# Keys of elements 0 and 1 and the values of element 0 of the third stage computed between the first attention and the FFN; the first gelu ahead of the last copy of transposed probabilities

## The reference

```python
x = x + _L0_xattn_ref(_layernorm(x), ctx_1024, ctx_1024, ...)      # 16 heads of 8, causal
x = x + _L0_ffn_ref(_layernorm(x), w_up, w_down)                   # 128 -> 512 -> 128, ternary weights, gelu
x = x + _L1_xattn_ref(_layernorm(x), ctx_1024, ctx_1024, mask, ...) # 16 heads of 64, relative positions
x = x + _L1_ffn_ref(_layernorm(x), rhs)                            # int8 product, 128 x 128
```

```python
hq = (q @ Wq).reshape(Bq, Lq, D_K, N_HEADS)
hk = (k @ Wk).reshape(Bq, Lk, D_K, N_HEADS)      # keys: from the context alone
hv = (v @ Wv).reshape(Bq, Lk, D_V, N_HEADS)      # values: from the context alone
attn = jnp.einsum('bidn,bjdn->bijn', hq, hk)
attn = attn + jnp.take_along_axis(b_full, idx[None, :, :, None], axis=2)   # relative positions
out = jnp.einsum('bijn,bjdn->bidn', softmax(attn), hv)
```

## Time and profile before

| what | value |
|---|---|
| median of 3 runs | 449.82 us (449.65 to 452.0) |
| span of the profiled execution | 447.1 us |
| mean granted clock of TensorE | 0.977 |
| PE busy | 412.8 us (92%) |
| DVE busy | 380.6 us (85%) |
| ACT busy | 377.9 us (85%) |
| POOL busy | 252.8 us (57%) |
| PE's share of the chain that ended last | 71% |

### The profile page before, as it was taken

How to read it: one execution, slowest core, us unless ns; L and a number is a source line. 1 busy time by engine, 2 the same in 40 slices (tenths; PEclk the granted TensorE clock), 3 DMA queues, 4 the chain that set the end, 5 groups by cost and what they waited for, 6 DMA issues and landing times.

```text
span 447.1 us, 16738 instructions
## 1 busy us (share of the span) xinstructions
PE 412.8 (92%) x6147; PEld 313.4 (70%) x6147; DVE 380.6 (85%) x1236; ACT 377.9 (85%) x1483; POOL 252.8 (57%) x370
## 2 busy tenths in 40 slices
PE   8999999998789998999999999999999999998771
PEld 6555565654457677877788888877888887887560
DVE  5799999989758984697779999998999999899954
ACT  1999999998945565599999999999999999999851
POOL 4388888887967651023345454644745555365765
PEclk9999999999979999999999999999999999999796
DMA  7250000000000002999667667666757847772000
GB/s 215 60 195 25 15 7 11 11 8 15 2 0 2 0 2 74 241 215 217 141 146 172 151 144 171 150 131 153 167 134 152 192 118 164 153 171 53 6 8 23
DMA packets 54392, 44.88 MB, mean 100 GB/s; under 512 B 43952, under 2 KB 49328, under 8 KB 54320
## 3 DMA queue, kind: packets, MB, share of 16 engines
q1 hardware_dynamic: 53616, 43.59, 41.1%
q10 hardware_dynamic: 704, 0.32, 0.3%
HBM read 22.92 MB, written 20.97 MB: 98 GB/s over the span
## 4 chain that ended last, share of the span: by engine, by line
PE 71%; DVE 17%; ACT 5%; issue 3%; POOL 2%; DMA 1%; SPq 1%; POOLq 0%; ACTq 0%; DVEq 0%
PE PS L1003 61%; PE PS L1213 4%; PE PS L1019 3%; PE PS L1179 1%; DMA wr<-in_wr 1%; DVE relr L753 1%; ACT prob L523 1%; DVE nmax L705 1%; DVE nmax L707 1%; POOL prob L320 1%; DVE relw L748 1%; DVE nmax L676 1%; DVE probT L683 1%; PE PS L1169 1%; DVE nmax L770 1%
## 5 line engine op out<-in xcount | busy, mean ns | idle before, releaser
L377 POOL TENSOR_TENSOR prob<-prob,rsum 128x480 f32<-128x480 f32 x64 | 66.4, 1057 | 83.1 <-DVE rsum L903 59.7
L523 ACT ACTIVATE prob<-prob,nmax 128x120 f32<-128x120 f32 x256 | 100.2, 417 | 1.8 <-DVE nmax L923 1.8
L439 ACT ACTIVATE prob<-PS,nmax 128x120 f32<-128x120 f32 x256 | 89.6, 393 | 4.2 <-DVE nmax L770 2.5
L320 POOL TENSOR_TENSOR prob<-prob,rsum 128x480 f32<-128x480 f32 x64 | 62.5, 988 | 22.8 <-DVE rsum L743 12.7
L439 ACT ACTIVATION_READ_ACCUMULATOR prob<-PS,nmax 128x1 f32 x256 | 61.2, 239 | 0.0
L523 ACT ACTIVATION_READ_ACCUMULATOR prob<-prob,nmax 128x1 f32 x256 | 56.8, 222 | 0.0
L1003 PE MATMUL PS<-xnT,wq 128*128 128x128 f32 x288 | 43.1, 286 | 2.2 <-ACT xnT L591 1.1
L1003 PE MATMUL PS<-rT,qv 64*32 64x152 f32 x2048 | 40.7, 292 | 2.5 <-issue 2.2
L1003 PE MATMUL PS<-probT,hv 120*64 120x128 f32 x512 | 36.0, 284 | 6.8 <-ACT probT L608 4.4
L1003 PE MATMUL PS<-ctx,wk 128*128 128x120 f32 x288 | 41.1, 279 | 0.0
L1003 PEld LDWEIGHTS PS<-probT,hv 120*64 120x64 f32 x512 | 28.0, 139 | 18.3 <-issue 8.0
(11 more groups left out here) (191 smaller groups left out, 1082.1 us busy)
## 6 DMA issues: line engine op xcount, KB each, us to landing
rel_scratch<-relw SPq DMA_DIRECT2D x128, 152.0 KB, 2.6
relr<-rel_scratch SPq DMA_DIRECT2D x64, 240.0 KB, 4.6
ctx<-in_ctxT SPq DMA_DIRECT2D x32, 60.0 KB, 1.9
out_x<-fin SPq DMA_DIRECT2D x16, 64.0 KB, 4.0
x_all<-in_x SPq DMA_DIRECT2D x1, 640.0 KB, 7.1
wr<-in_wr SPq DMA_DIRECT2D x1, 512.0 KB, 5.4
wq<-in_wq SPq DMA_DIRECT2D x1, 512.0 KB, 3.7
wk<-in_wk SPq DMA_DIRECT2D x1, 512.0 KB, 4.5
```

Source lines behind the costliest of these rows:

```text
L320: return pool.tensor_tensor(pr, pr, cols(rsum[p], g, HG).unsqueeze(2).to_broadcast([S, HG, SK]), ALU.mult)
L377: return pool.tensor_tensor(pr, pr, cols(rsum[p], g, HG).unsqueeze(2).to_broadcast([S, HG, SK]), ALU.mult)
L439: last = act.activation(cols(prob[p], n, SK), cols(scores, q, SK), ACT.Exp, bias=nmax[p][:, n:n + 1], accum_out=ssum[p][:, n:n + 1])
L523: last = act.activation(cols(pr, n, SK), cols(pr, n, SK), ACT.Exp, bias=bias[:, n:n + 1], accum_out=total[:, n:n + 1])
```

## The change

`made_early(t)` is true for elements 0 and 1. For these the key products and both copies of the keys leave `layer1`, and for element 0 the value products and copies leave it too. They are placed in `attn0(16)`, `ffn0(0)` and `attn0(17)` of the crossing, in banks that are free there (keys of element 0 in banks 2 and 3, of element 1 in banks 0 and 3; values in banks 1 and 3). Of the six copies of keys and values made there, three are on DVE and three on ACT. On ACT the gelu of FFN element 0 now stands inside `attn0(17)`, ahead of the copy of the last transposed probabilities. SP waits for `cap` as well before it loads a context and a mask, because the values of element 0 no longer tell it that the buffer is free. The core of the diff:

```diff
+        def made_early(t):
+            return isinstance(t, int) and t < 2
...
@@ SP, layer1
                     after(sp, A1["hv_ps"], 2 * t - 2)
+                    after(sp, A1["cap"], t - 1)
...
@@ ACT, attn0, ahead of the copy of probT_ps 2t+2 of element s-2
+                if at_step(s, NB + 1):
+                    act.wait_ge(A1["hv_ps"], 2)
+                    act.activation(cols(hv[0], 0, 512), PS[0:SK, 3, :], ACT.Copy).then_inc(A1["hv0"], 1)
+                    ffn0(0, 0)
+                    act.wait_ge(A1["hk_ps"], 3)
+                    act.activation(cols(kT[1], 1, 4 * SK), PS[:, 0, 0:4 * SK], ACT.Copy).then_inc(A1["kT1"], 1)
@@ ACT, crossing
                 ffn0(-1, 1)
+                act.wait_ge(A1["hv_ps"], 1)
+                act.activation(cols(hv[0], 1, 512), PS[0:SK, 1, :], ACT.Copy).then_inc(A1["hv1"], 1)
                 attn0(17, 1)
-                ffn0(0, 0)
                 attn0(18, 0)
@@ DVE, attn0, between the reciprocals of rsum
+                    if at_step(s, NB):
+                        dve.wait_ge(A1["hk_ps"], 1)
+                        dve.tensor_copy(cols(kT[0], 1, 4 * SK), PS[:, 2, 0:4 * SK]).then_inc(A1["kT1"], 1)
@@ DVE, attn0, ahead of the copy of oT
+                if at_step(s, NB):
+                    dve.wait_ge(A1["hk_ps"], 2)
+                    dve.tensor_copy(cols(kT[0], 0, 4 * SK), PS[:, 3, 0:4 * SK]).then_inc(A1["kT0"], 1)
+                if at_step(s, NB + 1):
+                    dve.wait_ge(A1["hk_ps"], 4)
+                    dve.tensor_copy(cols(kT[1], 0, 4 * SK), PS[:, 3, 0:4 * SK]).then_inc(A1["kT0"], 1)
@@ PE
+            def key_half(t, h, bank):
+                for m in range(4 * h, 4 * h + 4):
+                    last = mm(PS[:, bank, (m % 4) * SK:(m % 4 + 1) * SK], cols(wk1_sb, m, 2 * DK), ctx_sb[t][:, :])
+                last.then_inc(A1["hk_ps"], 1)
+            def value_half(t, h, bank):
+                mm(PS[0:SK, bank, :], ctx_sb[t][:, :], cols(wv1_sb, h, 512)).then_inc(A1["hv_ps"], 1)
@@ PE, attn0, after the product with wo
+                if at_step(s, NB):
+                    pe.wait_ge(attn1_loaded, 16 * 11)
+                    pe.wait_ge(A1["ctx_loaded0"], 16)
+                    pe.wait_ge(A0["probs"], 62)
+                    key_half(0, 1, 2)
+                if at_step(s, NB + 1):
+                    pe.wait_ge(A1["ctx_loaded1"], 16)
+                    pe.wait_ge(F0["xnT"], 1)
+                    key_half(1, 1, 0)
@@ PE, attn0, after the transposes of groups 2 and 3
+                if at_step(s, NB + 1):
+                    pe.wait_ge(A1["hv0"], 1)
+                    key_half(1, 0, 3)
@@ PE, attn0, between the two halves of probT x vexp
+                if at_step(s, NB):
+                    pe.wait_ge(A0["probs"], 64)
+                    key_half(0, 0, 3)
@@ PE, attn0, after the second half of probT x vexp
+                if at_step(s, NB):
+                    value_half(0, 1, 1)
@@ PE, ffn0, after the up product
+                if at_step(s, 0):
+                    pe.wait_ge(A1["kT0"], 1)
+                    value_half(0, 0, 3)
@@ PE, layer1 (four places, and the copies of ACT and DVE likewise)
-                    for m in range(4, 8):
+                    if not made_early(t):
+                        for m in range(4, 8):
```

More of the change, by code:

```diff
@@ L1306, in layer1 @@
                     freed(pe, (A1["relw2"], t + 2, t + 1), (A1["kT1"], t + 1, t))
[L1307 to L1309 removed]
+                    if not made_early(t):
+                        for m in range(0, 4):
+                            last = mm(PS[:, 4, (m % 4) * SK:(m % 4 + 1) * SK], cols(wk1_sb, m, 2 * DK), ctx_sb[p][:, :])
+                        last.then_inc(A1["hk_ps"], 1)
                 t, p = s - 4, par
```

33 lines of the change are left out of this document (19 added, 14 removed).

## The result

| | before | changed |
|---|---|---|
| median of 20 runs each | 449.9 us (447.24 to 455.26) | 452.47 us (451.12 to 457.0) |
| ratio to before | | 1.0066, 95% interval 1.0046 to 1.0087 |
| span of the profiled execution | 447.1 us | 451.6 us |
| its granted clock | 0.977 | 0.977 |

The changed kernel is slower by 0.66%. The forecast was 449.3 us and "within 0.5%"; 452.47 us lies above its range. The profiled execution of the changed kernel took 453.43 us, 1.8 us more than its span, and in every execution with both numbers on record the difference is 1.75 to 1.89 us. So the 2.7 us that I took for what lies around the program was wrong: the profiled execution of before took about 448.9 us, 1 us less than the median, and the profiled one of the changed kernel 1 us more than its own.

The account below looks back on a forecast made before the run. PE was taken to bound the crossing and the third stage's long middle, perhaps with `relw` transfers in its first steps. Span 447.1 + 0.5 - 1.0 = 446.6 us, plus 2.7 us, gave 449.3 us; range 448.0 to 452.0 us.

Parts of the forecast that it names:

- the third-stage term: First steps of the third stage: content products of element 1 start 1.0 us earlier, passed on to the end.
- My bounds: Third-stage gain: 0.1 us if the load at 197.25 us holds PE, 2.1 us if PE's lead is kept whole.
- the loads hold the third stage: Rival for the third stage: loads set the pace, gain only 0.1 us, time 450.2 us; chance 0.1.
- The crossing term: Between attention and FFN: 4.57 us of added PE work on the chain costs +0.5 us, with the clock at 2.4 GHz.
- POOL's wait: Crossing: element 15's transposes wait for POOL's scaling, which let PE start at 124.78 us; PE now comes at 125.13 us.
- the key group: Crossing: each group of key products on PE's chain was priced at 0.89 us at full clock.
- My upper bound: Crossing cost at full clock: +1.5 us, from 0.2 us of wait for each of five groups following a semaphore.
- the second rival: Crossing: the clock fall was absent from timed runs, so 2.2 us more cost, time 451.5 us; chance 0.2.
- the reading of the rows: Crossing: PE's idle pauses of 1.95 us preceded the clock's fall; with work filling them it stays up, giving 449.3 us.

Follow-up runs that it names:

- the filler: Kernel before plus four unread constant products (0.9 us) in PE's pause ahead of the crossing's transposes of element 14; ratios 0.992 and 0.9922 in two runs.
- Crossing only: Changed kernel with unread products of the same shapes put back in the third stage where the moved ones stood; 450.75 us, ratio 1.0012.
- The kernel with this pause filled: Changed kernel plus two unread products of 512 columns in PE's pause ahead of element 2's first position products; 449.79 us, ratio 1.0002.
- the third stage alone: Changed kernel with each moved product group in the crossing cut to one product of 16 or 32 columns; 451.5 us, ratio 1.0023.
- small loads: Changed kernel with only the loads of `relr` for elements 0 and 1 cut to one head in eight; 450.67 us, ratio 1.0022.
- small transfers: Kernel before and changed kernel, each with `relw` stores and `relr` loads of elements 0 and 1 cut to one head in eight; 451.03 and 449.79 us.
- the repeat: Kernel before, unaltered, profiled once more; this execution took 448.87 us, span 447.1 us.
- The two halves alone: Changed kernel with only its crossing products moved in, then with only its third-stage products removed; ratios 1.0012 and 1.0023.

## Why the prediction was wrong

**The failed step is the third-stage term, "-1.0 us, passed on".** Measured at element 2 it is +0.4 to +0.6 us (40.59, 40.65 and 40.76 in three profiles of the changed code against 40.17 and 40.18 us), an error of 1.5 us. Before's code with the filler was once at 40.17 and once at 40.59 us, so the sign of 0.4 us is weak; that there is no gain of 1.0 us is clear. Two assumptions fell.

I let the position products of element 2 start 0.5 us earlier, because I kept the landings of `relr` at their old times. They started 0.2 us later: 21.55 us after the first query products, where before has 21.37. DVE's line 999 started on the landing of a load at 189.94 us, 19.25 us after those products, where its line 974 started at 18.77 us before, because SP issued the load's pair 1.3 us later, behind a store whose last packets had stood behind a transfer of instructions. Crossing only has the same lateness with all its products in place (0.9 us at element 2), so this part of the loss is not owed to the products that I had moved out of the stage.

And I took PE's pause ahead of those products (I had written 1.2 us; it is 2.46 us) as free of cost, when a pause of 1.95 us had brought half clock 70 us earlier in my own argument. The kernel with this pause filled prices the clock at 0.9 us at element 1. It also shows that the gain there need not be passed on: with `ctx` late, element 2 gives nothing back. My bounds, 0.1 to 2.1 us of gain, did not reach a loss at all, and the rival "the loads hold the third stage" had the wait, with the clock missing from it. The gain itself was not invented: 1.74 us of lead at element 0 with the third stage alone, 1.0 us at element 1 with small loads, 3.0 us passed on with small transfers in both kernels.

**The crossing term was right in kind and too small.** Clock 1.00, gelu at nothing, copies in time, POOL's wait met: all as written. From the transposes to the end I had 10.11 us and it was 10.42 us. The term that was too small is the key group: the three on the chain take 0.98 to 1.08 us from start to start here, where I had 0.89 us from the third stage, in which products of the same shape follow; that is 0.47 us more, and the other rows give 0.16 us back. My upper bound had such time as waits.

**The base was not the constant that I made it.** I priced 4.57 us of work at +0.5 us because full clock gives back what half clock took. That holds against an execution with the fall. Against one without it, 7.79 us, the crossing costs 2.63 us. I had this as the second rival, with 2.2 us for the fall, where it measures 1.74 us, and chance 0.2; the repeat shows it true of some executions. How many of the timed ones is not known. What I held against that rival, that span and median agree if 2.7 us lies around the program, was no evidence, since 1.8 us does.

**Not in the sum at all: the long steps of the middle.** They add 1.3 us in the first pair of profiles, 0.8 us in the second (187.07 and 187.27 against 185.74 and 186.48 us). They belong to the program and not to the execution, since they return at the same two steps in four profiles, and they move or vanish with edits elsewhere. The traces tie them to the transfers of instructions: nineteen stalls of nineteen end 1.17 to 1.53 us after a packet of the instruction queue. The Trainium skill, page "Runtime: NRT & Kernel Launch", section "Instruction fetch mechanics", says that each engine's instructions are fetched in blocks ahead of use, which is mostly hidden, and that a taken branch out of the fetched blocks stalls the engine. The trace agrees that there are such transfers, most of them without a stall; here the stalls that do come are 0.4 to 2.0 us long, and whether PE stood still for its next block, and whether the loop's branch has to do with it, no run here decides.

**The sum.** The median is 3.2 us above the forecast. Third stage 1.5, crossing 0.3, middle 0.8 to 1.3, in all 2.6 to 3.1 us. What the executions of before without a fall add would come on top, so it does not close exactly, and a falling clock in the start (1.6 us in the changed profile, 3 us in its repeat, none in both of before) is of unknown weight: it was in five of the eight profiles whose crossing holds key or value products at full size, and in none of the six others. I count that as a suspicion. The two halves alone give 1.0012 and 1.0023, which add to 1.0035; the whole is 1.0066. Neither half has a long step, where the changed kernel has 2.05 us of them and before 0.75 us or more; with both put in, (2.05 + 0.75)/450 = 0.0062, the halves make 1.0097. Third stage only has its stall of 2.03 us, which the changed kernel has not; without it they make 1.0052. Each of them is uncertain by 0.003, so this only shows that nothing large is missing.

The rule that I had set against the rows (the page "TensorE: Matmul & The Clock Gate" of the Trainium skill, Part 1: the clock goes down after a window in which PE was idle) can now be judged. With the pause filled or lessened the clock was 1.00 in the crossing in ten profiles of ten, with the pause open it fell in three of four. So work in the pause does seem to prevent the fall, which speaks for the reading of the rows; that it failed to come once fits the page's remark that the window runs free of the program.

## What to carry to other kernels

Work that is moved out of a stage which waits for transfers leaves a pause there, and the pause gives back no time and can cost clock: ask of each place that loses work what PE will do in its stead, not only of each place that gains it. And a landing time read from one program is no constant for the next: here one packet of instructions in another place made it 0.5 us later. Before spending real work on a pause, put a few constant products into it and time that: here 0.9 us of them gained 0.8%, about half of it by luck in other stages, where the real work cost 0.7%. And where an edit is worth half a per cent, compare profiles stage by stage and repeat them, because stages that nobody touched moved by 1 to 5 us.

## What the runs showed that I had not expected

- The same program, with the same pause of PE, kept the clock in one execution and lost it in another: crossing 7.79 and 9.53 us.
- PE stalls in the middle of a group of products, on no semaphore, at the same instructions in every profile of a kernel: 0.90, 1.15 and 0.87 us near 369 us in three profiles of the changed code. Nineteen such stalls of 0.42 to 2.03 us all end 1.17 to 1.53 us after a transfer of instructions. A few products added 180 us earlier took them away, in before and in the changed kernel alike.
- One 16 KB packet of instructions held the last two packets of a store back, in five profiles of five in which it began before the store had ended, and the load behind it was issued at 14.1 to 14.7 us instead of 12.7 to 13.1 us.
- Two unread products on PE, 1.9 us of work, brought the next content products forward by 1.1 us.
